# The first attention's core: a loop of twelve turns written out as straight code

## The reference

```python
q = (x @ w_q.T).reshape(b, s, H, HD)
k = (x @ w_k.T).reshape(b, s, H, HD)
v = (x @ w_v.T).reshape(b, s, H, HD)
q = _apply_rope(q, cos, sin)
k = _apply_rope(k, cos, sin)
att = jnp.einsum('bqhd,bkhd->bhqk', q, k) / jnp.sqrt(jnp.asarray(HD, x.dtype))
att = jax.nn.softmax(att, axis=-1)
y = jnp.einsum('bhqk,bkhd->bqhd', att, v).reshape(b, s, H * HD)
return y @ w_o.T
...
x = x + _layernorm(_L0_attn_ref(_layernorm(x, axis=-1), L0_attn_w_q, L0_attn_w_k, L0_attn_w_v, L0_attn_w_o), axis=-1)
x = x + _layernorm(_L0_ffn_ref(...), axis=-1)
```

## Time and profile before

| | us |
|---|---|
| median of 3 runs | 4434.79 |
| lowest, highest run | 4431.49, 4459.29 |
| span of the profiled execution, from its first to its last instruction | 4390.4 |
| core of the first attention in it, from its first exponential on | 144.8 to about 850 |
| core of the last attention in it | 3371 to about 4121 |

### The profile page before, as it was taken

The page is one execution under the profiler, slowest core; times in us unless marked ns, Lnnn a source line. Parts: engine busy times, 40 slices in busy tenths (PEclk is TensorE's granted clock), DMA queues, the critical chain, the costliest instruction groups (busy, mean ns, idle before and its releaser), DMA issues. The chain is left out here.

```text
span 4390.4 us, 103771 instructions
## 1 busy us (share of the span) xinstructions
PE 4026.2 (92%) x39404; PEld 2157.8 (49%) x39412; DVE 3325.7 (76%) x5684; ACT 2853.6 (65%) x4554; POOL 1999.5 (46%) x1895
## 2 busy tenths in 40 slices
PE   8899999988959947799999999999999999999987
PEld 4344444464537622344545445454454555555555
DVE  7888999676654559888888888887227888888686
ACT  5567777664543245688887888876125777777674
POOL 5122222251224646788888888877000222222332
PEclk9899999999978979799999999999998999999999
DMA  5211111105223435464555655555224222222100
GB/s 146 62 36 37 36 36 39 28 21 130 70 101 116 120 101 132 110 166 139 155 159 155 163 144 152 159 145 149 91 67 131 59 69 63 59 69 62 32 11 29
DMA packets 263654, 411.63 MB, mean 94 GB/s; under 512 B 52635, under 2 KB 139706, under 8 KB 263074
## 3 DMA queue, kind: packets, MB, share of 16 engines
q1 hardware_dynamic: 233478, 376.07, 30.8%
q0 software_dynamic: 6912, 18.88, 1.7%
q10 hardware_dynamic: 22848, 11.02, 1.0%
HBM read 351.85 MB, written 53.24 MB: 92 GB/s over the span
## 5 line engine op out<-in xcount | busy, mean ns | idle before, releaser
L2966 POOL TENSOR_TENSOR l_dbx<-l_u,l_bc 128x1024 f32<-128x1024 f32 x256 | 603.3, 2357 | 254.1 <-DVE banks L3487 86.9
L1170 DVE CUSTOM_DVE_ANT_0 banks<-banks,l3s_table 128x1024 f32<-128x1024 f32 x512 | 619.8, 1240 | 95.3 <-PE banks L1090 90.2
L1253 ACT ACTIVATE l3s_probs<-banks 128x512 f32<-128x512 f32 x1024 | 541.8, 595 | 224.7 <-PE banks L1090 117.5
L1165 DVE TENSOR_REDUCE l0s_peak<-banks 128x1 f32<-128x1024 f32 x512 | 605.5, 1213 | 78.3 <-PE banks L1090 77.4
L1253 ACT ACTIVATE l0s_probs<-banks 128x512 f32<-128x512 f32 x1024 | 536.3, 601 | 185.0 <-PE banks L1090 183.0
L3274 ACT ACTIVATE banks<-l_dt,l_decay 128x512 f32<-128x512 f32 x512 | 346.7, 687 | 224.8 <-DVE banks L3487 222.2
L2976 POOL TENSOR_TENSOR l_ys<-l_ys,l_hc 128x1024 f32<-128x1024 f32 x203 | 479.6, 2363 | 22.3 <-DVE l_hc L3498 22.1
L3148 PE MATMUL banks<-l_ha,l_ring 128*128 128x512 f32 x1024 | 446.7, 593 | 4.0 <-issue 4.0
L3148 PE MATMUL banks<-l_hb,l_ring 128*128 128x512 f32 x1024 | 444.8, 595 | 1.6 <-ACT l_hb L3239 0.8
L3487 DVE TENSOR_TENSOR_SCAN banks<-banks,l_carry,l_dbx 128x512 f32<-128x512 f32 x256 | 319.3, 1278 | 68.4 <-ACT banks L3274 61.9
L1090 PE MATMUL banks<-l3s_q_st,l3s_k_st 122*32 122x512 bf16 x4096 | 348.8, 382 | 11.2 <-DMA l3s_q_st<-l3s_nm_rows 7.3
(11 more groups left out here) (525 smaller groups left out, 7231.9 us busy)
## 6 DMA issues: line engine op xcount, KB each, us to landing
l_bc<-l_bc_rows SPq DMA_DIRECT2D x256, 512.0 KB, 5.4
l_ring<-in_l2f_stream SPq DMA_DIRECT2D x176, 512.0 KB, 6.5
l3s_table<-bias_table SPq DMA_DIRECT2D x16, 960.0 KB
qk_parts<-l0s_probs SPq DMA_DIRECT2D x96, 128.0 KB, 2.4
qk_parts<-l3s_probs SPq DMA_DIRECT2D x32, 384.0 KB, 3.5
y_rows<-l1f_out_b SPq DMA_DIRECT2D x80, 128.0 KB, 1.7
l0s_q_st<-qk_parts SPq DMA_DIRECT2D x64, 96.0 KB
l0s_k_st<-qk_parts SPq DMA_DIRECT2D x64, 96.0 KB
```

Source lines behind the costliest of these rows:

```text
L1165: nc.vector.tensor_reduce(out=peak[:, b % 2, t:t + 1], in_=s1[t % 2], axis=AX, op=ALU.max, negate=True).then_inc(s1_used, 1)
L1170: nc.vector.tensor_tensor_reduce(out=s1[t % 2], in0=s1[t % 2], in1=rows, scale=1.0, scalar=LOW, op0=ALU.add, op1=ALU.max, accum_out=peak[: ...
L1253: nc.scalar.activation(columns(probs[b % 2][:, t, :], half * 512, (half + 1) * 512), scores, ACT.Exp, scale=scale).then_inc(s2_used, 1)
L2966: nc.gpsimd.tensor_tensor(dbx[:, at:at + 2], u[:, 2 * mh:2 * mh + 2], bc[:, load % BR, 0].unsqueeze(1).to_broadcast([P, 2, TB]), ALU.mult)\
```

## The change

`steps` loses its loop. The middle items of both attentions are now written out as straight code, as those of the last attention already were, and `steps` and its five calls lose the parameter that named the engine. Nothing else is changed: the order of steps, the buffers and the semaphores are the same, and the waits have the same values. The code of the last attention's core stays as it was.

```diff
-        def steps(eng, step):
+        def steps(step):
...
             step(1, 1, "ab23l")
-            for m in range(2, 5):
+            for m in range(2, items - 11):
                 step(m, m % PERIOD, "ab23ln")
-            if bias:
-                for m in range(5, items - 11):
-                    step(m, m % PERIOD, "ab23ln")
-            else:
-                with eng.Fori(0, (items - 16) // PERIOD) as i:
-                    for m in range(5, 5 + PERIOD):
-                        step(PERIOD * i + m, m % PERIOD, "ab23ln")
             for m in range(items - 11, items - 3):
                 step(m, m % PERIOD, "ab23ln" if m == items - 8 else "ab23l")
...
-            steps(pe, step)
+            steps(step)
```

More of the change, by code:

```diff
@@ L1082, in step @@
                     load_bias(head_of(it, m) + 1, 1 - m // BATCH)
-            steps(sp, step)
+            steps(step)
         @block.tensor
@@ L1192, in step @@
                         maximum(*job)
-            steps(v, step)
+            steps(step)
         @block.gpsimd
@@ L1240, in step @@
                     cut_maximum(it + 1, (m + 1) % PERIOD)
-            steps(g, step)
+            steps(step)
         @block.scalar
@@ L1259, in step @@
                         exponential(it, m, slot // 2, slot % 2)
-            steps(act, step)
+            steps(step)
 class TernaryMlp:
```

## The result

The changed kernel takes 4374.94 us (median; 4368.22 to 4380.06), the kernel before 4434.07 us (4431.49 to 4459.29). The ratio is 0.985, with a 95% interval of 0.982 to 0.988: 59 us faster, three times the 19.1 us that were forecast, and outside the range. It is what rival (e) named, faster by over 44 us, to which the prediction gave a chance of 0.03.

The account below looks back on a forecast made before the run. TensorE was taken as the bound in the first attention's core; jumps back gave 19.1 us, register work and fetching 0, so 4434.8 - 19.1 = 4415.7 us, 0.43% less, with a range of 4404 to 4432 us.

Parts of the forecast that it names:

- rival (e): Looped items: much faster, over 44 us, needing 0.5 us off each of 48; chance 0.03 together with unseen causes.
- Part 2: All five sequencers: computed waits and addresses become constants, the other four engines' branches go; worth 0, within 0.8 us.
- Part 3: Eight quick turns: code must be fetched all the way, net 45 packets more; price 0, up to 3.7 us for the range.
- (b): The other loop's taken branch: moved code makes it miss, one stall of at most 7.1 us, 4422.8 us; chance 0.08.
- (d): Four small DMAs carrying the maxima: fetches delay them, 19.3 us slower, 4454.1 us; chance 0.05.
- the sum's: Whole kernel: span 4390.4 less 19.1 us, plus 44.4 us of median above span taken as untouched, gives 4415.7 us.
- Part 1: First attention's core: TensorE's jumps back go, so the stalls of three slow turns vanish; 19.1 us less.
- The sum for eleven jumps: First attention's loop: were all eleven taken jumps to stall, 11 x 6.4 = 70 us; set against 19.1 us to be had.

Follow-up runs that it names:

- e2_pe_straight: TensorE's stream alone made straight code, the other four engines keep the loop, against the kernel before: 4380.1 us, ratio 0.9974.
- e3_pe_loop: TensorE keeps the loop, the other four engines made straight code, against the kernel before: 4401.4 us, ratio 1.0036.

## Why the prediction was wrong

**The bound and the mechanism were right.** TensorE sets the pace, its jumps back in the first three turns stalled, and straight code removed just that: 19.7 us of 22.0 between the two profiles. Register work and the other engines' branches are worth nothing (Part 2), shown for the core by `e2_pe_straight` and `e3_pe_loop`, and by loops without a long branch whose core takes 665.2 us. Fetching all the way costs nothing (Part 3): 39 packets more in the page, the same 42.8 us for four items. Rivals (b) and (d) didn't come: the branch of line 48 is at most 0.25 us in every profile, and the matmuls lose 0.6 us to the four small DMAs, though the loads wait for them more often.

**The step that failed is the sum's**: "The runs' median stands 44.4 us above the span, a part that the change has no reason to touch". The right part is about 2 us, as every result since shows. No trace was kept of an execution of the kernel before at 4434 us, but all that the runs show says that the other 42 us were the same stalls again: its execution with seven long branches took 4418.1 us, the moved loop with eleven 4453.9, and on the chip where its median was 4436.1 us the move by 96 instructions left 4378.8. Part 1's term, 3 jumps at 6.4 us, had the price nearly right (6.5 to 7.1 us in the kernel before and with TensorE alone looped, 8.3 only where the loop was moved) and the count wrong: it was read from one execution, and it varies: 1, 3 and 7 in three profiles of the same program, and by its quickest and slowest runs from none to ten or all eleven. Part 1 should have said 6.5 us times a count between 0 and 11. Worked back from the time, these runs had the three seen and (4434.8 - 4392.2) / 6.5 = 6.6 more, some 62 us; as the count comes from the time itself, that this lies near the 59 measured is no proof of it. The sum for eleven jumps, 70 us, stood in the prediction and was set aside because rows 2 hold only 19.1, and rival (e) was judged by the pace of the matmuls in the same execution. Two signs were passed over: the sum left 44 us without a place, and of why the body is held from the fourth jump on the prediction said that "the forecast doesn't need it", which is the very thing that decides the count.

**What decides the count.** Shown: it depends on how much code the body has (1637 instructions of TensorE's stream: none to eleven; 1253: none; 3270: all five) and on where it starts (moved by 32 instructions: all eleven; by 64, 96 and 120: none; by 0 and 8: a count that varies). A long turn fetches nine packets, a quick one none. Once a jump has found its target no later one is long, so in the five profiles that have both kinds the long turns come first and in one piece.

Shown as well is what the instruction queue does at the jumps. In the profiles of the kernel before, of TensorE alone looped and of 16 waits, a packet's fetch begins with every long branch: within 0.1 us of the branch's start for 13 of the 18, and 0.6 to 0.8 us behind it for the others. The nearest fetch to the first quick branch begins 6 us ahead of it. With 64 waits a fetch begins some 0.6 to 0.7 us ahead of every branch, and every branch is long. But with 128 and 192 waits one begins 0.6 us ahead of the first branch too, and that branch is quick.

Argued: a packet holds 256 instructions (the straight kernel's stream of TensorE, some 80,700 instructions, comes in 314 packets, 257 to a packet), so 1637 are 6.4 packets and touch seven or eight, depending on the start. The fetch runs ahead of the execution; if it reaches past the loop's end, what it brings in may take the place of the loop's first packet. Near the edge, a race between that fetch and the jump would give a varying count. The fetches that begin together with the long branches fit a race, but no run shows which packet is displaced, nor where the body starts.

The expectations took touching eight packets for the cause, and a start 120 to 150 instructions into a packet. With the moves as they really were the two don't go together: moved by 64 or 96 instructions such a body would touch eight, and no branch was long there. A start of 192 to 223 fits all runs: eight packets in the kernel before and with 16 and 64 waits, seven with the others. Eight packets are then held as long as the ninth isn't fetched ahead of the jump, which is decided by how far the body reaches into the eighth. One thing in the traces favours this. Where the loop was held with 128, 192 and 240 waits, the packet fetched ahead of the first jump isn't fetched again in the loop, and behind its last branch the next fetch begins only after 4.5 to 5.7 us; in the kernel before and with 16 waits it begins after 1.2 to 1.7 us. So the packet behind the body seems to be held beside a body of seven, and not beside one of eight. It is a reading of the queue's times all the same: the start itself is shown nowhere.

The Trainium skill, Advanced Engine Details and Errata, section "ISA Cache", gives TensorE 128 KB in lines of 16 KB with 256 instructions. From this follow eight lines, as an estimate, though the same section says that there are only two. The runs contradict two: a body of 6.4 packets is held for eight turns without one fetch. Eight fits them: the 12.8 packets of 3270 instructions were held at no jump, and the account above counts on eight. They don't prove the number.

The same program had medians of 4434, 4395, 4436 and 4386 us in four sets of runs, the last three on three chips (the first one's isn't on record). Each set was one chip at one time, so whether the chip or something else that differed decides stays open.

## What to carry to other kernels

Here a hardware loop on TensorE is free if its body stays in instruction memory and costs 6.5 to 8.3 us a turn if it doesn't; near the edge 32 instructions ahead of it make every turn pay and 64 none, and in between one profile shows one draw of a distribution. Whoever moves code by an edit should count the move in the trace: here it was half the number of waits written. Before a count that is read from a profile goes into a sum, compare that execution's own time with the other runs; a gap between span and median that no row fills is a finding, not a constant. Straight code isn't the only cure here (128 waits in an idle place gave the same core time), but it has no jump back that could miss, wherever it lies.

## What the runs showed of the hardware

TensorE's taken branch takes 0.21 to 0.24 us where its target is held, those of the other engines 0.04 to 0.07 us; a branch that must fetch takes 3.3 to 5.0 us, and the rest of its price comes after it. In the run with 64 waits the jumps are shorter (3.5 to 3.9 us) than in the kernel before (4.1 to 5.0 us), yet each costs more, 8.3 against some 6.5 us. Its turn from 288.2 to 338.8 us is 7.8 us longer than one whose target is held; 4.8 us of it are idle time, and the busy time is 3.0 us more, as TensorE works at the lower clock. The idle time is two stalls by issue: 3.13 us at the jump, and 1.63 us more 2 us later:

```profile
292.52 0.40 PE L1093 MATMUL banks<-l0s_q_st,l0s_k_st 98*32 98x512 bf16 x4 [3.13 <-issue]
...
295.19 1.04 PE L1093 MATMUL banks<-l0s_q_st,l0s_k_st 98*32 98x512 bf16 x7 [1.63 <-issue]
```

The turn of the kernel before at 240.3 has 4.6 us of idle time, nearly all of it in one stall, and 1.8 us more of busy time. So the stall at the jump is shorter with 64 waits, and what makes the turn dearer is the second stall and how long the granted clock stays at 1.2 GHz behind them: 6.8 to 10.2 us in its turns, 3.4 or 6.8 us in those of the kernel before.
